# Expert stage of a routed feed-forward layer: 71 groups of 128 slots in place of 39 groups of 256

## The reference

```python
gate_logits = x_flat @ gate_w.T                      # (4096, 8)
topk_vals, topk_idx = jax.lax.top_k(gate_logits, 2)
topk_w = jax.nn.softmax(topk_vals, axis=-1)
...
for e in range(8):
    h = gelu(x_flat @ w1[e].T + b1[e])               # 256 -> 1024
    y = h @ w2[e].T + b2[e]                          # 1024 -> 256
    out = out + comb[:, e:e + 1] * y                 # weight 0 for 6 of the 8 experts
```

## Time and profile before

| | |
|---|---|
| median of 3 runs | 1756.46 us (1754.28 to 1761.42) |
| span of the profiled execution, first to last instruction | 1730.5 us |
| median less that span (start and end of the program) | 26.0 us |
| PE busy over the span | 1401.0 us, 81% |
| DVE, ACT, POOL busy | 905.9, 766.9, 237.7 us |
| mean granted TensorE clock | 0.900 |

### The profile page before, as it was taken

How to read it: one execution, slowest core, us unless ns; L and a number is a source line. 1 busy time by engine, 2 the same in 40 slices (tenths; PEclk the granted TensorE clock), 3 DMA queues, 4 the chain that set the end, 5 groups by cost and what they waited for, 6 DMA issues and landing times. The chain is left out here.

```text
span 1730.5 us, 29759 instructions
## 1 busy us (share of the span) xinstructions
PE 1401.0 (81%) x10104; PEld 1085.0 (63%) x10105; DVE 905.9 (52%) x1670; ACT 766.9 (44%) x1419; POOL 237.7 (14%) x200
## 2 busy tenths in 40 slices
PE   4989898956597879878887887666089999999993
PEld 3877776745335643664366346665079999999982
DVE  4746364615657564665466553776035555555541
ACT  3444343415666756665676562335032332332321
POOL 0000000000000000000000000017513333333332
PEclk9999999978798989898998998558589999999996
DMA  7600000030000000000000001529322333333326
GB/s 227 134 25 1 25 0 24 0 99 30 1 14 1 13 26 14 1 13 27 14 1 19 7 1 29 167 77 361 75 75 49 48 49 49 49 49 47 45 32 206
DMA packets 79035, 91.67 MB, mean 53 GB/s; under 512 B 16608, under 2 KB 70368, under 8 KB 78816
## 3 DMA queue, kind: packets, MB, share of 16 engines
q1 hardware_dynamic: 62400, 63.39, 12.5%
q0 software_dynamic: 16544, 27.08, 8.0%
HBM read 48.89 MB, written 41.56 MB: 52 GB/s over the span
## 5 line engine op out<-in xcount | busy, mean ns | idle before, releaser
L2132 ACT ACTIVATE moe_hid<-moe_hbank,moe_b1T 128x256 f32<-128x256 f32 x312 | 130.7, 470 | 283.2 <-PE moe_hbank L2082 283.1
L2082 PE MATMUL moe_hbank<-moe_xT,l_w1T 128*128 128x256 f16 x1872 | 212.9, 274 | 0.0
L2097 PE MATMUL moe_ybank<-l_w2T,moe_hid_hi 128*128 x1248 | 206.4, 273 | 0.0
L2082 PEld LDWEIGHTS moe_hbank<-moe_xT,l_w1T 128*128 x1872 | 182.7, 98 | 21.6 <-issue 0.3
L2048 POOL DMA_INDIRECT acc_scratch<-moe_y,moe_meta x78 | 149.0, 1910 | 306.4 <-DVE moe_y L2167 284.4
L1062 ACT ACTIVATE block_probs<-block_bank 128x1024 f32<-128x1024 f32 (+1 forms) x192 | 144.5, 808 | 75.3 <-PE block_bank L798 74.6
L2097 PE MATMUL moe_ybank<-l_w2T,moe_hid_lo 128*128 x624 | 170.1, 273 | 0.0
L2097 PEld LDWEIGHTS moe_ybank<-l_w2T,moe_hid_hi 128*128 128x128 f16 x1248 | 122.1, 98 | 14.1
L2153 DVE TENSOR_SCALAR moe_hid_hi<-moe_hid 128x2048 f16<-128x2048 f32 x39 | 47.8, 1227 | 153.1 <-ACT moe_hid L2132 153.1
L1390 DVE TENSOR_TENSOR block_probs<-block_probs,block_mask 128x512 f32<-128x512 f32 x64 | 44.2, 691 | 118.6 <-ACT block_probs L1062 118.3
L820 PE MATMUL block_bank<-block_probs,block_v 128*32 128x512 f32 (+3 forms) x768 | 86.1, 521 | 23.6 <-DVE block_probs L1390 23.3
(11 more groups left out here) (339 smaller groups left out, 2948.9 us busy)
## 6 DMA issues: line engine op xcount, KB each, us to landing
route_natural<-in_L_ffn_w SPq DMA_DIRECT2D x32, 512.0 KB, 6.1
rows_scratch<-l_blank SPq DMA_DIRECT2D x2, 5031.0 KB, 33.6
moe_xin<-rows_scratch SPq DMA_DIRECT2D x39, 258.0 KB, 2.7
l_xs<-in_x SPq DMA_DIRECT2D x8, 512.0 KB, 7.9
x_scratch<-l_xs SPq DMA_DIRECT2D x4, 1024.0 KB, 4.0
block_xin<-x_scratch SPq DMA_DIRECT2D x16, 256.0 KB, 3.1
acc_scratch<-block_res SPq DMA_DIRECT2D x16, 256.0 KB, 2.2
route_tok<-acc_scratch POOLq DMA_DIRECT2D x4, 1024.0 KB, 7.3
```

The lines of the kernel that those rows point to most:

```text
L2082: last = pe.matmul(hbank[:, c, :], w1T[:, e, wp, k, c * P:(c + 1) * P], xT[q][:, xp, k, :], start=n == 0, stop=n == 5)
L2097: last = pe.matmul(ybank[q][:, t, :], (hid_hi, hid_lo)[hp][q][:, c, t * P:(t + 1) * P], w2T[:, e, wp, c, :], start=n == 0, stop=n == 3 * H ...
L2132: act.activation(hid[q][:, c, :], hbank[:, c, :], ACT.Gelu, bias=b1T[:, e, c:c + 1], scale=1.0 / (GAIN * GAIN)).then_inc(S["gelu_done"], 1)
```

## The change

GT becomes 1: a group has 128 slots, and there are 64 + 7 = 71 groups (9088 slots) in place of 32 + 7 = 39 groups (9984 slots). Everything with a GS or GT in its shape halves: the moving operand of `up` has 128 columns, ACT's and DVE's instructions of a group work on half the elements, and a group has one scatter. The PSUM tiles are given the size of whole banks, so that two chunks still share a bank and no more than two. Two scratch tiles of `route` (`cmp`, `cmp_s`) grow with GROUPS and move into `tok[0]`, which is free by then.

```diff
--- before.py
+++ after.py
@@ -1642,7 +1642,7 @@
 TILES = B * T // P
 TOPK = 2
 
-GT = 2
+GT = 1
 GS = GT * P
 GROUPS = TILES * TOPK // GT + E_N - 1
 ROW = 2 * D + 4
@@ -1686,12 +1686,13 @@
         iota_s = s.sb("iota_s", [1, GROUPS])
         within, total = s.sb("within", [P, TILES, E_N]), s.sb("total", [P, TILES, E_N])
         scan = s.sb("scan", [P, 2, TILES, E_N])
-        cmp = s.sb("cmp", [P, E_N, TILES // GT])
+        cmp = tok[0][:, 2:3, 0:E_N * TILES // GT].rearrange("p a (e t) -> p (a e) t", e=E_N)
         groups_e = s.sb("groups_e", [P, E_N])
         esc = s.sb("esc", [P, 2, E_N])
         posf, pos = s.sb("posf", [P, TILES]), s.sb("pos", [P, TOPK, TILES], U32)
         diff, wt = s.sb("diff", [P, TILES]), s.sb("wt", [P, TOPK, TILES])
-        cmp_s, sum_s = s.sb("cmp_s", [1, GROUPS, E_N - 1]), s.sb("sum_s", [1, GROUPS])
+        sum_s = s.sb("sum_s", [1, GROUPS])
+        cmp_s = tok[0][0:1, 0:2, :].rearrange("p a d -> p (a d)")[:, 0:GROUPS * (E_N - 1)].rearrange("p (s e) -> p s e", e=E_N - 1)
 
         wbank = [s.ps(f"wbank{i}", [P, 512]) for i in range(4)]
         xbank = [s.ps(f"xbank{i}", [P, 512]) for i in range(2)]
@@ -2000,9 +2001,14 @@
         hid_lo = [s.sb(f"hid_lo{i}", [P, HC, GS], F16) for i in range(2)]
         y = [s.sb(f"y{i}", [P, GT, D]) for i in range(2)]
         ysum = [s.sb(f"ysum{i}", [P, GT, D]) for i in range(2)]
-        turned = s.ps("turned", [P, 2 * CC, GS], F16)
-        hbank = s.ps("hbank", [P, HC, GS])
-        ybank = [s.ps(f"ybank{i}", [P, GT, D]) for i in range(2)]
+        turned = s.ps("turned", [P, 1024], F16)[:, 0:2 * CC * GS].rearrange("p (n q) -> p n q", q=GS)
+        hbank = s.ps("hbank", [P, HC // 2, 512])
+        ybank = [s.ps(f"ybank{i}", [P, 512])[:, 0:GT * D].rearrange("p (t d) -> p t d", d=D) for i in range(2)]
+
+        def hidden(c):
+
+            return hbank[:, c // 2, c % 2 * GS:(c % 2 + 1) * GS]
+
         names = ("bias_loaded", "in0", "in1", "turned_full", "xT_done", "h_full", "gelu_done", "hi_done", "lo_done", "y_full",
                  "meta_done", "ysum_done", "y_done", "added", "passed")
         S = {n: s.sem(n) for n in names}
@@ -2079,7 +2085,7 @@
                         n = 0
                         for wp, xp in ((0, 0), (0, 1), (1, 0)):
                             for k in range(CC):
-                                last = pe.matmul(hbank[:, c, :], w1T[:, e, wp, k, c * P:(c + 1) * P], xT[q][:, xp, k, :],
+                                last = pe.matmul(hidden(c), w1T[:, e, wp, k, c * P:(c + 1) * P], xT[q][:, xp, k, :],
                                                  start=n == 0, stop=n == 5)
                                 n += 1
                         if c % 2 == 1:
@@ -2129,7 +2135,7 @@
                         act.wait_ge(S["lo_done"], j - 1)
                     for c in range(HC):
                         act.wait_ge(S["h_full"], j * (HC // 2) + (c // 2 + 1))
-                        act.activation(hid[q][:, c, :], hbank[:, c, :], ACT.Gelu, bias=b1T[:, e, c:c + 1],
+                        act.activation(hid[q][:, c, :], hidden(c), ACT.Gelu, bias=b1T[:, e, c:c + 1],
                                        scale=1.0 / (GAIN * GAIN)).then_inc(S["gelu_done"], 1)
 
                 all_tiles(act, step)
```

## The result

The change makes the kernel slower: 1910.45 us (median of 4 runs, 1908.44 to 1915.71) against 1758.6 us, a ratio of 1.0853 (95% interval 1.0818 to 1.0887), so +151.9 us. Forecast were 1921 us, or +164.5. The profiled span is 1908.3 us. A run's time is 1.7 us longer than its own span (1909.99 and 1908.3 here), so the 26.0 us in the table of the kernel before are not the start and end of the program: its profiled execution was a shorter one than the timed runs. The forecast adds its difference to the median of the runs, so this does it no harm.

What follows compares the result with a forecast made beforehand. PE's array bounds the expert stage before, PE's sequencer after: +165.8 us there, -2.0 at the tail and +0.7 in `route` make +164.5 on 1756.5, so 1921 us. The 8-in-10 range was 1876 to 1970 us.

Steps and rivals of the forecast that it cites:

- The bound moves to PE's sequencer: Expert stage: PE's sequencer, at 8.34 us a group, sets the step instead of the array, which needs 5.5 us.
- 8.34 us a group: Expert stage: the sequencer's summed work per group; 71 groups make 592.1 us against 426.3, so +165.8 us.
- It costs nothing before: Expert stage of the kernel before: the sequencer's register instructions cost nothing, hidden behind the array's 10.93 us step.
- Tail, -2.0 us: After the last `down`: the last scatter goes out 2.9 us behind it instead of 4.94, so -2.0 us.
- `route`, +0.7 us: In `route`: DVE's chain ahead of the scatters gets longer, as `cmp`, `cmp_s` and their reductions grow: +0.7 us.
- The scatter loop at 5.8 us: Expert stage rival: `meta` waiting for an earlier scatter sets a 5.8 us step, 1743 us; chance 0.07 with the array.
- The array at 5.5 us: Expert stage rival: PE's array sets a 5.5 us step, 1722 us; chance 0.07 together with the scatter loop.
- The rival that weight loads bind the 128-column matmuls: Expert stage: weight loads of 98 ns, none hidden, make 7.7 us a group and 1876 us; chance 0.04.
- the 81 ns a pair: Expert stage: the page's time per weight load and 128-column matmul gives 6.8 us a group, near 1813 us.
- The clock: Expert stage rival: PE's granted clock falls; at 0.80 the step is 9.4 us and the time 1996 us; chance 0.07.

Runs made afterwards that it cites:

- the fixed expert there: The kernel before, with PE using expert 0's weights for every group, so no expert reads or register instructions: 1725.74 us, ratio 0.9987.
- without the middle pass: The changed kernel without the second of `up`'s three passes (high weights times low tokens): 1881.69 us, ratio 1.0874.
- fixed expert, meta copy behind `out`: The changed kernel with expert 0's weights for every group on PE and DVE's copy of the meta data moved behind `out`: 1690.54 us, ratio 0.9796.
- the second profile: The changed kernel run again with no edit, beside the kernel before on one chip: 1879.53 us, ratio 1.0865.

## Why the prediction was right, by its steps

- **The bound moves to PE's sequencer.** Shown three ways. Taking a third of `up`'s matmuls out changes nothing (stage 584.9). Taking three in four of `down`'s reads out gains 47 us (538.2). And with the scatter loop out of the way (588.3 by itself), taking out `up`'s register instructions and its read brings the step down to the array's (396.8).
- **8.34 us a group.** Measured 8.18 in the mean. By terms, from the rows above: `up` 4.1 (forecast 4.1), on to `down` 0.9 (0.95), `down` 1.9 (1.95), to the next `up` 1.2 (0.12 + 1.1, by the next step's first matmul at 1425.05 less 0.1). This step has no branch; with it the loop's mean is 8.24, so 0.1 us a group was too much, 7 us in all. The rest of the 11 us between 165.8 and 154.7 is mostly the stage's first step, which has no `down` and takes 5.2 us, and which the sum took at full length.
- **It costs nothing before.** Shown by the ratio 0.9987 of the fixed expert there.
- **Tail, -2.0 us.** The last scatter goes out 3.35 us behind the last `down` (1870.81; POOL's row starts at 1874.16), against 4.94: -1.6.
- **`route`, +0.7 us.** From DVE's copy of `within` to POOL's first scatter of rows it is 9.50 us (1144.87 to 1154.37), against 8.73 before (1150.92 to 1159.65): +0.8.
- **The scatter loop at 5.8 us.** The mechanism was right as the next bound and the size was wrong: 7.1 to 7.2 us. The terms of the earlier trace rows were read where nothing waits: the read on DVE was 0.6 us too short and the landing 0.8. Had the sequencer been free, the forecast of that rival, 1743 us, would have been wrong, and the change still slower (ratio 1.045).
- **The array at 5.5 us.** 5.52, once both other bounds are gone. The rival that weight loads bind the 128-column matmuls falls with it, and so do the 81 ns a pair of the Trainium skill, page "TensorE: Matmul & The Clock Gate", section "Back-to-back issue gap": 52 pairs with 128 columns and 24 with 256 take 5.52 us in all, and with 109 ns for each of the 24 that leaves 56 ns for each of the 52.
- **The clock.** In the changed kernel it stayed at 0.99 over the stage, with PE standing still for 0.65 us at a time, so the forecast held here. It fell to 0.92 without the middle pass, where by the rival's way of reckoning (16% of the time at the lower level, a step of 9.2 us of array work there against 8.2) the stage should have grown by some 12 us, an estimate. It did not grow. Some steps there are 9.4 to 10.3 us and the ones behind them 6.2 to 7.3, so the array catches up; the rival was priced too high.

## What to carry to other kernels

Each new weight address that depends on a register brings a register instruction, and these come 0.13 us apart, more than the 0.109 us of a matmul with 256 columns. Count both streams, the array's and the sequencer's, before making tiles smaller: the array's shrinks with the tile and the sequencer's does not. Where two loops lie close together above the bound, an edit that frees one shows a part of its worth or nothing; take both out before judging either.

## What the hardware did that was not expected

- Handing on matmuls costs the sequencer hardly anything: between two register instructions there may be one matmul or three, and 32 of them take 4.1 us either way (32 matmuls or 48 in `up`).
- Scatters beside 1 MB copies in SBUF landed in 4.8 us in the median, against 3.9 with the same order of work and no copies (fixed expert, meta copy behind `out`) and 3.7 in the changed kernel. Those that began 1.2 to 1.5 us ahead of a copy's issue took 6.7 us and more.
- In the first profile of the changed kernel, the engines stand idle for up to 10.6 us at a time in `route`'s weight loops while POOL scatters, and the stage begins 30 us later than in the second. The waits between 1085 and 1285.4 us, chief row:

```profile
PE route_wbank L1821 <- issue: 49.2, 7, 10.1
```

PE's idle time ahead of these matmuls is 88.3 us in all there, 24.3 in the second profile and 23.7 in the kernel before. The timed runs beside the first were 31 us longer for both kernels than in the later comparisons (1758.6 and 1910.45 against 1727.73 and 1879.53), so the difference between the kernels is the same. What causes the late waits, and whether they make up those 31 us in the kernel before as well, stays open.
